# A float32 attention-and-MLP kernel: the exp(s) transposes go to the slot scores' bank and ahead of the probability transposes, and two PSUM banks get fixed roles

## The reference

```
x = layernorm(hidden)                                  # [8, 256, 256]
q, k, v, g = heads of x @ Wq.T, Wk.T, Wv.T, Wg.T       # 16 heads of 128
q, k = rope(q), rope(k)
s  = clip(x @ Ws1.T @ Ws2.T + bs2, -32, 32)            # 64 slots a head
es = exp(s);  enz = exp(-cumlogsumexp(s, over time))
A  = tril(q @ k.T) / sqrt(128)
ok = enz * (A @ es)                                    # [t, 64]
p  = softmax(ok)
W2 = tril((p * enz) @ es.T)
o  = rmsnorm(W2 @ v) * g_norm * silu(g)
attn = o @ Wo.T
mlp  = (gelu(x @ Wgate.T) * (x @ Wup.T)) @ Wdown.T     # 4-bit weights, dequantised
out  = hidden + attn + mlp
```

## Time and profile before

| | |
|---|---|
| time before | median 1188.34 us of 3 runs (1185.62 to 1189.64) |
| profiled execution | 1186.13 us, its span 1184.4 us |
| PE busy | 1114.7 us, 94% of the span |
| DVE, ACT, POOL busy | 80%, 54%, 35% |
| granted TensorE clock, mean | 0.986 of full speed |

### The profile page before, as it was taken

One profiled execution on the slowest core, in us unless ns is written; L12 is line 12 of the kernel. 1 busy time (PEld: TensorE's weight loads), 2 busy tenths in 40 slices (PEclk: granted clock), 3 DMA queues, 4 the chain that ended last, 5 costly groups with the idle time before them and its releaser, 6 DMA issues.

```text
span 1184.4 us, 20879 instructions
## 1 busy us (share of the span) xinstructions
PE 1114.7 (94%) x6872; PEld 941.6 (79%) x6872; DVE 943.1 (80%) x1808; ACT 642.1 (54%) x1748; POOL 419.6 (35%) x306
## 2 busy tenths in 40 slices
PE   6789999999999998999989999899998999999995
PEld 5568888888788887888878888788887888788884
DVE  6888887888868887888877888778886888877763
ACT  5355564655645565555655556464563565655451
POOL 5233242433513335232443324343251433523231
PEclk9899999999999999999999999999999999999998
DMA  4001000100001000010000100001000100000001
GB/s 157 1 1 74 1 1 1 52 22 1 1 2 73 1 1 2 1 73 1 1 3 1 74 1 1 3 16 59 1 1 2 73 1 1 1 2 19 1 19 36
DMA packets 9117, 23.19 MB, mean 20 GB/s; under 512 B 816, under 2 KB 5808, under 8 KB 7984
## 3 DMA queue, kind: packets, MB, share of 16 engines
q1 hardware_dynamic: 9008, 21.76, 5.0%
HBM read 19.66 MB, written 2.10 MB: 18 GB/s over the span
## 4 chain that ended last, share of the span: by engine, by line
PE 71%; issue 8%; DVE 6%; ACT 6%; POOL 3%; POOLq 0%; DVEq 0%; ACTq 0%
PE bank L203 17%; PE bank L205 16%; PE bank L204 16%; PE bank L292 5%; ACT xs L568 3%; PE bank L305 3%; PE bank L349 2%; DVE xs L860 2%; POOL qkT L1087 2%; PE bank L294 2%; DVE Wt L740 2%; ACT xs L567 2%; PE bank L282 1%; PE bank L338 1%; PE bank L341 1%
## 5 line engine op out<-in xcount | busy, mean ns | idle before, releaser
L1096 POOL TENSOR_TENSOR inter_lo<-ffb,inter_hi 128x512 fp32r<-128x512 f32 x64 | 83.3, 1323 | 433.2 <-ACT inter_hi L617 433.2
L1087 POOL TENSOR_TENSOR qkT<-ra,xs 128x512 f32<-128x512 f32 x128 | 163.5, 1277 | 95.1 <-DVE xs L860 67.6
L586 ACT ACTIVATE sm<-bank,mx 128x64 f32<-128x64 f32 x256 | 76.3, 325 | 168.5 <-DVE mx L816 168.5
L857 DVE TENSOR_TENSOR ra<-bank,rope 128x512 f32<-128x512 f32 x128 | 88.0, 687 | 55.1 <-ACT xs L568 54.9
L805 DVE RECIPROCAL enzT<-enzT 128x256 f32<-128x256 f32 x64 | 111.6, 1744 | 0.0
L860 DVE TENSOR_TENSOR xs<-xs,rope 128x512 f32<-128x512 f32 x128 | 109.0, 852 | 0.0
L203 PE MATMUL bank<-xh,wqk_hi 128*128 128x512 f32 x256 | 107.4, 420 | 0.0
L203 PE MATMUL bank<-xh,wgu_hi 128*128 128x512 f32 x256 | 106.9, 418 | 0.0
L591 ACT ACTIVATE At<-bank 128x128 f32<-128x128 f32 x128 | 35.4, 276 | 132.0 <-DVE At L740 132.0
L205 PE MATMUL bank<-xh,wgu_lo 128*128 128x512 f32 x256 | 101.6, 397 | 0.0
L203 PE MATMUL bank<-wvg_hi,xh 128*128 128x512 f32 x256 | 101.4, 396 | 0.0
(11 more groups left out here) (137 smaller groups left out, 3211.5 us busy)
## 6 DMA issues: line engine op xcount, KB each, us to landing
raw<-in_w_qkvg SPq DMA_DIRECT2D x8, 1024.0 KB, 4.9
scaled<-in_w_scaled SPq DMA_DIRECT2D x8, 640.0 KB, 7.7
packed<-in_w_packed SPq DMA_DIRECT2D x8, 384.0 KB, 5.4
acc<-in_x SPq DMA_DIRECT2D x4, 512.0 KB, 8.6
out<-acc SPq DMA_DIRECT2D x4, 512.0 KB, 3.0
ws_raw<-in_w_slot SPq DMA_DIRECT2D x8, 48.0 KB, 1.8
rope<-in_rope_tab SPq DMA_DIRECT2D x1, 256.0 KB, 7.0
osq<-in_w_slot SPq DMA_DIRECT2D x1, 128.0 KB, 3.3
```

Source lines behind the costliest of these rows:

```text
L857: dve.tensor_tensor(two(ra[i % 2][:, :]), two(pj[i][:, :]), cos, ALU.mult).then_inc(cos_done, 1)
L1087: pool.tensor_tensor(qkT[:, i, :], ra[i % 2][:, :], xs[i % 2][:, :], ALU.add).then_inc(roped, 1)
L1096: pool.tensor_tensor(inter[1][e][:, :], ffb[e][:, :], inter[0][e][:, :].bitcast(F32), ALU.subtract).then_inc(inter_lo, 1)
```

## The change

The transposes of the next stage's es move from their place between values 0 and values 1 to a place between output half 1 and v/g projection 3. Their copy on ACT moves from between the two squares at the stage's end to just ahead of the exponentials of the softmax. E now goes to bank 4, the one that S has had; K goes to bank 5. A tiles take the banks 4, 5, 4, 5 in every stage, W tiles as well. The waits that protect the banks change with that: score tiles 0 and 1 wait for the third and fourth W copy (score tile 1 waited for J_ready), and the first slot weights wait for J_ready in place of A_off and clip_done.

```diff
@@ pe: slot_scores, scores, slot_rows, slot_weights
-                pe.matmul(sc_bank((bp - 1) % BP, "S")[:, :] if n is not None else sc[1][:, :],
+                pe.matmul(sc[0][:, :] if n is not None else sc[1][:, :],
-                dst = sc_bank(bp, "A", i)
+                dst = sc[b]
-                dst = sc_bank(bp, "K")
+                dst = sc[1]
-                pair = [(sc_bank(bp, "W", 2 * b + h), slice(h * M, (h + 1) * M)) for h in range(2)]
+                pair = [(sc[h], slice(h * M, (h + 1) * M)) for h in range(2)]
@@ pe: stage
                 for i in (0, 1):
-                    if first and i == 1:
-                        pe.wait_ge(clip_done, 1)
-                    elif first or i == 1:
-                        pe.wait_ge(J_ready, st + 1)
+                    if first:
+                        pe.wait_ge(clip_done if i == 1 else J_ready, 1)
                     else:
-                        pe.wait_ge(W_off, 4 * st)
+                        pe.wait_ge(W_off, 4 * st - 1 + i)
                     scores(st, bp, i, hp)
...
-                slot_rows(st, bp)
+                slot_rows(st)
                 if not first:
                     outputs(st, 1, php, st + 1)
+                if not last:
+                    pe.wait_ge(es_ready, st + 2)
+                    slot_transpose(sc[0], esT[nbp % 2])
                 if not last:
                     project_vg(st + 1, nbp, nhp, 3, True)
                 pe.wait_ge(p_ready, st + 1)
...
                 pe.wait_ge(qe_ready, st + 1)
-                pe.wait_ge(A_off, 4 * st + 4)
-                if not last:
-                    pe.wait_ge(clip_done, st + 2)
+                if not last:
+                    pe.wait_ge(J_ready, st + 2)
                 slot_weights(st, bp, 0)
...
                 values(st, bp, 0)
-                if not last:
-                    pe.wait_ge(es_ready, st + 2)
-                    pe.wait_ge(W_off, 4 * st + 3)
-                    slot_transpose(sc_bank(bp, "E", 0), esT[nbp % 2])
@@ act: stage
-                softmax_exp(st, bp)
+                if not last:
+                    copy_J(st + 1, sc[0][:, :])
+                softmax_exp(st)
...
                 square_o(st, 0)
-                if not last:
-                    copy_J(st + 1, sc_bank(bp, "E", 0)[:, :])
                 square_o(st, 1)
```

More of the change, by code:

```diff
@@ L56 @@
 W_VG, W_QK, W_GU, W_OD = range(4)
-SC_SLOTS = {"A": (0, 1, 2, 3), "S": (4,), "K": (5,), "W": (6, 7, 8, 9), "E": (10,)}
-SC_STEP = 11
 def build(nc, x, w_qkvg, w_packed, w_scaled, w_slot, w_slot1, g_norm, rope_tab, out):
@@ L186, in tokens @@
                 bp * TOK + tile * P, bp * TOK + (tile + 1) * P)
-        def sc_bank(bp, kind, i=0):
-            return sc[(SC_STEP * bp + SC_SLOTS[kind][i]) % 2]
         def each_stage(eng, stage):
@@ L309, in slot_reads, with slot_rows @@
                 mm.then_inc(ok_full, 1)
-            def slot_rows(st, bp):
+            def slot_rows(st):
                 pe.wait_ge(okz_done, st + 1)
-                dst = sc_bank(bp, "K")
+                dst = sc[1]
                 for i in range(NT):
@@ L577, in copy_J, with softmax_exp @@
                 act.activation(esJ[:, :, :].rearrange("p n m -> p (n m)"), src, ACT.Copy).then_inc(J_ready, 1)
-            def softmax_exp(st, bp):
+            def softmax_exp(st):
                 act.wait_ge(mx_done, st + 1)
@@ L582, in softmax_exp @@
                 wait(act, rs_done, st)
-                src = sc_bank(bp, "K")
+                src = sc[1]
                 for g in range(8):
@@ L587, in softmax_exp, with off_diagonal @@
                 ins.then_inc(p_ready, 1)
-            def off_diagonal(diag, done, dst, bp, kind, st, i, scale):
+            def off_diagonal(diag, done, dst, st, i, scale):
                 act.wait_ge(diag, 4 * st + i + 1)
-                act.activation(dst[i][:, 1, :], sc_bank(bp, kind, i)[:, P:2 * P], ACT.Copy,
+                act.activation(dst[i][:, 1, :], sc[i % 2][:, P:2 * P], ACT.Copy,
                                scale=scale).then_inc(done, 1)
@@ L662, in stage @@
                 npar = (bp + 1) % 2
-                a_args = (A_diag, A_off, At, bp, "A", st)
-                w_args = (W_diag, W_off, Wt, bp, "W", st)
+                a_args = (A_diag, A_off, At, st)
+                w_args = (W_diag, W_off, Wt, st)
                 more = not (isinstance(hp, int) and hp == HP - 1)
@@ L734, in two, with diagonal @@
                 return ap.rearrange("p (b t) -> p b t", b=2)
-            def diagonal(full, done, dst, bp, kind, st, i, mask, used):
+            def diagonal(full, done, dst, st, i, mask, used):
                 dve.wait_ge(full, 4 * st + i + 1)
                 wait(dve, *used)
-                src = sc_bank(bp, kind, i)[:, 0:3 * P].rearrange("p (n t) -> p n t", n=3)
+                src = sc[i % 2][:, 0:3 * P].rearrange("p (n t) -> p n t", n=3)
                 dve.tensor_tensor(dst[i][:, 0:3:2, :], src[:, 0:3:2, :], mask[:, :, :], ALU.mult).then_inc(done, 1)
@@ L811, in softmax_in, with softmax_max @@
                 dve.tensor_tensor(okz[:, :], rg[0][:, :], enzT[par][:, :], ALU.mult).then_inc(okz_done, 1)
-            def softmax_max(st, bp):
+            def softmax_max(st):
                 dve.wait_ge(K_full, st + 1)
                 wait(dve, p_ready, st)
-                dve.tensor_reduce(mx[:, :], sc_bank(bp, "K")[:, :].rearrange("p (g m) -> p g m", m=M),
+                dve.tensor_reduce(mx[:, :], sc[1][:, :].rearrange("p (g m) -> p g m", m=M),
                                   AX_X, ALU.max, negate=True).then_inc(mx_done, 1)
@@ L947, in stage @@
                 more = not (isinstance(hp, int) and hp == HP - 1)
-                a_args = (A_full, A_diag, At, bp, "A", st)
-                w_args = (W_full, W_diag, Wt, bp, "W", st)
+                a_args = (A_full, A_diag, At, st)
+                w_args = (W_full, W_diag, Wt, st)
                 if bp == 3 and more:
@@ L977, in stage @@
                 if not last:
-                    clip(st + 1, npar, sc_bank(bp, "S")[:, :])
+                    clip(st + 1, npar, sc[0][:, :])
                 if not first:
@@ L993, in stage @@
                     invert(st + 1, npar, 0)
-                softmax_max(st, bp)
+                softmax_max(st)
                 if not first:
```

## The result

The changed kernel takes 1251.99 us (median of 4 runs, 1249.72 to 1254.77), against 1186.98 before (1185.38 to 1189.64): a ratio of 1.0546, 95% interval 1.0515 to 1.0578. It is slower by 65 us, where 1257 with a range of 1237 to 1280 was predicted. The profiled execution took 1251.35 us.

A forecast was written before the change was run, and what follows sets the result against it. PE was taken as the bound, a stage being PE's own length plus its waits. 63.3 - 0.3 + 4.2 + 3.4 = 70.6 us on 1186.1 gave 1257 us, forecast's own range 1243 to 1268, overall 1237 to 1280.

The forecast's parts named there:

- Steps 1 to 3: Middle of the stage: E at 524.58, esJ copy 0.67 us behind, exponentials 0.60 later, P 2.41 us late, waiting 2.05.
- Step 1: Middle of the stage: E starts at 524.58, its four transposes take 0.36 us, and PE reaches P at 526.33.
- Steps 4 and 5: First swap, rope and W copies 2.41 us late; values 1 start at 538.51, so each stage grows by 2.11 us.
- The two small terms: Additions beside the stall: 4.2 us for DVE's decode with bp 1, 3.4 us for clock falls with bp 3.
- The decode term: In seven stages with bp 1, DVE's later decode delays rope's first product by 0.6 us more, 4.2 us in all.
- The clock term: With bp 3 the end wait grows by some 0.3 us; two added clock falls, 3.4 us (bounds 0 and 12).
- this rival: The clock falls at the new stall before P too: 15 us (1271) in part, 51 us (1308) in every stage; chance 0.17.
- Rival 2: At the stage's end the rope chain makes good 0.57 us; the stage grows by 1.54, 46 us in all, 1240; chance 0.09.
- Rival 3: ACT's esJ copy runs in its 6.35 us idle time, E 2.4 us earlier; each stage gains 0.30, 1177; chance 0.02.
- Rival 4: No change to be seen: the softmax delay (3.2 us) lies inside the spare time at P (0.8 us); chance 0.02.

The follow-up runs named there:

- the run with a stall of 3.05 us: The changed kernel with E moved further back, behind v/g projection 3: 1329.04 us against 1187.14 for the kernel before, ratio 1.1166.
- the last run: Kernel before with fixed bank roles, plus q/k projection 0 ahead of P, and on ACT hidden high halves ahead of tile 3's v/g copies: 1175.38 us, ratio 0.9894.
- the first experiment: The changed kernel with the four es transposes (E) ahead of output half 1 instead of behind it: 1196.87 us against 1189.51 before, ratio 1.0067.

## Why the prediction was right

**The mechanism.** The exponentials stand in ACT's queue behind a copy that waits for E, and E waits for PE to come through output half 1. The profile after shows it directly, and two runs set it apart: one call moved on ACT alone gives 56 of the 65 us back, and 1.4 us more of the same wait makes an undisturbed stage 1.3 to 1.4 us longer.

**Steps 1 to 3.** E started 21.13 us into the stage, where 524.58 - 503.45 = 21.13 was predicted, the copy 0.64 behind it (0.67), the exponentials 0.50 behind the copy's start, not 0.60: the rows of these two ACT instructions overlap by 0.1 us, as those of the last exponential and the copy of v did before (525.14 and 525.00 in the earlier trace rows). They took 2.46 us, and P came 0.05 behind (2.47 and 0.06). P was 2.26 us late, not 2.41, and its idle time 1.65, not 1.9. Step 1 has E too cheap, 0.36 us where PE's next start is 0.44 behind it; that cost nothing here, since P waited anyway.

**Steps 4 and 5.** The first swap was 2.35 us late (2.41 predicted), the last W copy 2.46, and the stage 2.17 longer (2.11). In those 21 of the stages 1 to 30 whose clock stayed full in both traces the growth is 2.11 us on the mean. That it agrees so well is in part luck: in stage 13 P came 0.15 us less late than predicted, but the delay grew by 0.20 from P to the last W copy, where the prediction carried it on unchanged. From the first score matmul of stage 1 to that of stage 31 the trace of before has 1054.43 us, that of after 1118.58: 64.15 more, all but 1.1 of the 65.2 that the span grew.

**The two small terms.** The decode term, 0.6 us in each stage with bp 1, is all but absent: these stages grew by 2.15 us on the mean, those with bp 2 by 2.08. It was mis-sized through a duration that was itself a wait, as the last section shows. The clock term, two falls or 3.4 us, has the right sign and is too large: five places in the loop part have the lower clock, two of them for 6.8 us and three for 3.4, against four of 3.4 before; but part of it lies in idle time, and stage 16 had the same 0.95 in both. The fourteen stages with bp 3 or 0 grew by 2.17 us on the mean and the sixteen others by 2.12, so the clock's part is below 1 us. The sum was 70.6 us and came to 65.2 in the span; without the decode term it would have been 66.4.

**The rivals.** The clock didn't fall at the stall before P; the run with a stall of 3.05 us shows that it would have with a longer one, so this rival fell by size, not by kind. The Trainium skill, TensorE: Matmul & The Clock Gate, section on HAM oscillation, tells of repeated DMA waits of about 3 to 5 us that each bring the clock down again. The run with the wait of 3.05 us agrees in 25 of its 30 stages; the changed kernel's 1.65 us is shorter than the waits told of there, so the prediction carried that case over to a wait that it does not cover. Rival 2, an end of the stage that takes part of the delay up, is refuted: values 1 still waited 0.62 us for the last W copy. Rival 3 named the place of E at which the loss ends. With E there the exponentials start only 0.20 us later than before, where the changed kernel has 3.05, and the 0.3 us at values 1 are gained; but E's 0.44 us on PE ahead of P delays the swap by 0.43 and outweighs them, and each stage is 0.16 us longer, not 0.30 shorter. E at its old place filled a time in which PE waits anyway. The prediction's "PE's 0.36 us would vanish in the wait for W" was wrong: that wait is for the chain which P and the swap begin, and it moves with them. Rival 4, no change to be seen, fell with P's delay of 2.26 us.

## What to carry to other kernels

Before an instruction is moved ahead in an in-order queue, ask when its own input comes, not how long it takes: a copy of 0.6 us held up the softmax by 3 us because its producer stood behind 24 matmuls on another engine. Small work of the busiest engine belongs where that engine waits for a chain of the others; moved out of that gap, it delays the head of the same chain. And price the clock with the length of the wait: here the clock never fell behind 30 waits of 1.65 us, nor behind seven of 1.72 in the last run; it fell at two of seven of 2.02 to 2.12 in the kernel before, at six of seven of 2.25 to 2.34 in the first experiment, and at 25 of 30 of 3.05, which cost some 36 us beside the waits themselves.

## What the runs showed of the hardware

The decode on DVE (128x768 int32) had a row of 1.23 us before and of 0.65 after, with nothing changed in it. It overlaps the subtraction of 128x512 tiles on POOL, two instructions in one row. Before, in stage 13, beside the decode at 527.92:

```profile
527.43 2.84 POOL L1096 TENSOR_TENSOR inter_lo<-ffb,inter_hi 128x512 fp32r<-128x512 f32 x2 [14.82 <-ACT inter_hi L617]
```

and after, with the decode's row first:

```profile
556.29 0.65 DVE L858 TENSOR_SCALAR packed<-packed 128x768 int32<-128x768 int32 x1
555.22 2.85 POOL L1087 TENSOR_TENSOR inter_lo<-ffb,inter_hi 128x512 fp32r<-128x512 f32 x2 [17.27 <-ACT inter_hi L608]
```

The decode's end is 1.72 us behind POOL's start in both, whenever it began itself. With E ahead of output half 1 it is 532.72 + 1.33 - 532.34 = 1.71, and with the copy behind the exponentials 533.11 + 1.00 - 532.40 = 1.71. POOL's first instruction takes 1.30 of that, so the decode ends 0.42 us behind it. In the last experiment, where it begins beside the second of the two, it ends 0.42 us behind the second. This holds in all nine traces, for each of their eight rows of this decode: it ends 0.41 to 0.43 us behind the end of the POOL instruction that ran when it began, and its own row is between 0.55 and 1.34 us long. The decode's next step, the same operation on the same shape with nothing on POOL beside it, takes 0.54 to 0.55 each time. So the decode seems to be held until POOL's instruction is through, and to run the rest after it; a row of DVE beside a busy POOL can hold waiting time, and must not be carried to another moment. The Trainium skill, GPSIMD Engine Reference, section Specifications, says that POOL's SBUF interfaces are shared with VectorE, with contention for DVE instructions that run in a 2-port perf mode or have two SBUF inputs. The decode has one input, and no row shows in which mode it ran; its rows agree with such a contention, and no run was made to set it apart.
